# The expert's label read once per sequence on the sync engine's queue, in place of four times

## The reference

```python
x = x + L0(x)   # y = einsum('bnh,boh->bno', x, W[subject]) + b[subject]
x = x + L1(x)   # zX * second difference along features + zY * the same along tokens + zR * x * (1 - x)
x = x + L2(x)   # attention: 16 heads of 16, side input as queries, keys and values of x and one own key, then Wo
x = x + L3(x)   # experts, below
```

```python
s0 = relu(x @ swi[0]) @ swo[0]              # two shared experts, the same for every sequence
s1 = relu(x @ swi[1]) @ swo[1]
wi_sel = wi[type_label]                     # the chosen expert: one of five, its label is 0 to 2 here
wo_sel = wo[type_label]
h = relu(einsum('bsd,bdf->bsf', x, wi_sel)) # 256 x 1024
eo = einsum('bsf,bfd->bsd', h, wo_sel)      # 1024 x 256
w = softmax(relu(concat(eo[:, 0], s0[:, 0], s1[:, 0]) @ g1) @ g2)
return eo * w[0] + s0 * w[1] + s1 * w[2]
```

## Time and profile before

| | |
|---|---|
| Time, median of 3 runs | 972.61 us (971.57 to 976.15) |
| The profiled execution | 973.26 us |
| Its span in the profile | 971.4 us |
| Mean granted TensorE clock | 0.979 of full speed |
| Busy: TensorE / ScalarE / VectorE / GpSimd | 95% / 77% / 76% / 64% |
| DMA: mean rate | 154 GB/s |

### The profile page before, as it was taken

One profiled execution on the slowest core, in us unless ns is written; L12 is line 12 of the kernel. 1 busy time (PEld: TensorE's weight loads), 2 busy tenths in 40 slices (PEclk: granted clock), 3 DMA queues, 4 the chain that ended last, 5 costly groups with the idle time before them and its releaser, 6 DMA issues.

```text
span 971.4 us, 28400 instructions
## 1 busy us (share of the span) xinstructions
PE 923.5 (95%) x9138; PEld 891.7 (92%) x9138; DVE 734.1 (76%) x1518; ACT 751.3 (77%) x1682; POOL 625.1 (64%) x576
## 2 busy tenths in 40 slices
PE   8788999999999999999999999999999999999897
PEld 7688899999999999999999999999999999998897
DVE  6775777868877787887878788787878878788554
ACT  4777869688796978979697887969788796979552
POOL 4877657676675767667576766758666675866440
PEclk9999999999999999999999999999999999999999
DMA  6998867666677676667666676776767677676930
GB/s 189 199 175 189 141 174 152 157 157 132 180 154 176 138 159 160 135 173 155 179 141 157 157 140 173 149 174 152 157 157 140 173 151 176 149 157 124 148 94 11
DMA packets 361503, 149.47 MB, mean 154 GB/s; under 512 B 282340, under 2 KB 360452, under 8 KB 361476
## 3 DMA queue, kind: packets, MB, share of 16 engines
q1 hardware_dynamic: 361044, 148.74, 68.3%
q10 hardware_dynamic: 432, 0.39, 0.1%
HBM read 52.59 MB, written 4.20 MB: 58 GB/s over the span
## 4 chain that ended last, share of the span: by engine, by line
PE 62%; SPq 11%; DVE 7%; DMA 7%; ACT 6%; issue 5%; POOL 2%; ACTq 0%; DVEq 0%
PE out L760 7%; PE out L761 7%; PE out L762 7%; PE hid L760 6%; PE hid L762 6%; PE hid L761 6%; SPq L629 5%; PE front L760 4%; PE front L762 4%; PE front L761 4%; PE front L870 3%; DMA ksT<-parts_own 3%; DMA turned_own<-parts_own 3%; ACT prob_own L1131 3%; PE pv L827 2%
## 5 line engine op out<-in xcount | busy, mean ns | idle before, releaser
L1649 POOL TENSOR_TENSOR parts_own<-prob_own,parts_own 128x512 f16<-128x512 f32 x133 | 158.0, 1188 | 133.2 <-ACT parts_own L1137 133.0
L760 PE MATMUL hid<-x_hi,exp_hi 128*128 128x256 f32 x768 | 232.8, 303 | 5.5 <-DVE x_lo L1422 5.4
L1315 DVE TENSOR_REDUCE neg_max<-front 128x2 f32<-128x512 f32 x244 | 164.8, 687 | 85.3 <-PE front L870 82.8
L760 PE MATMUL out<-hid_hi,exp_hi 128*128 128x256 f32 x768 | 226.1, 294 | 2.3 <-ACT e_out L1160 2.3
L762 PE MATMUL hid<-x_hi,exp_lo 128*128 128x256 f32 x768 | 221.8, 289 | 0.0
L761 PE MATMUL hid<-x_lo,exp_hi 128*128 128x256 f32 x768 | 221.7, 289 | 0.0
L761 PE MATMUL out<-hid_lo,exp_hi 128*128 128x256 f32 x768 | 214.1, 279 | 0.0
L762 PE MATMUL out<-hid_hi,exp_lo 128*128 128x256 f32 x768 | 214.0, 279 | 0.0
L1131 ACT ACTIVATE prob_own<-front,neg_max 128x256 f32<-128x256 f32 x476 | 198.0, 482 | 13.0 <-DVE neg_max L1315 9.9
L1579 POOL TENSOR_TENSOR exp_lo<-raw,exp_hi 128x512 fp32r<-128x512 f32 x128 | 170.7, 1345 | 26.5 <-ACT exp_hi L1153 26.5
L1426 DVE SCALAR_TENSOR_TENSOR hid_lo<-hid,hid_hi 128x512 fp32r<-128x512 f32 x192 | 130.6, 686 | 48.0 <-ACT hid_hi L1175 45.8
(11 more groups left out here) (268 smaller groups left out, 2173.1 us busy)
## 6 DMA issues: line engine op xcount, KB each, us to landing
raw<-in_wi SPq DMA_DIRECT2D x64, 256.0 KB, 3.8
raw<-in_wo SPq DMA_DIRECT2D x64, 256.0 KB, 2.9
q_rows<-w_raw SPq DMA_DIRECT2D x80, 128.0 KB, 3.7
k_rows<-x_raw SPq DMA_DIRECT2D x48, 128.0 KB, 2.4
k_rows<-x1T SPq DMA_DIRECT2D x45, 128.0 KB, 2.4
x_raw<-in_x SPq DMA_DIRECT2D x16, 256.0 KB, 3.3
w_raw<-in_w SPq DMA_DIRECT2D x16, 256.0 KB, 2.7
s_raw<-in_side SPq DMA_DIRECT2D x16, 256.0 KB, 3.5
```

Of the source, the lines that this page charges most:

```text
L760: nc.tensor.matmul(acc, w_hi, a_hi, start=first, stop=False)
L1315: nc.vector.tensor_reduce(neg_max[:, :, h:h + 1], psum, AX_X, ALU.max, negate=True).then_inc(max_done, 1)
L1649: nc.gpsimd.tensor_tensor(of_head[:, 2 * S:4 * S], slot_of(prob, more_prob, i, h), of_head[:, 0:2 * S], ALU.subtract).then_inc(prob_split_ ...
```

## The change

A name `label` is added ahead of T0 in SP's list of the loop and of the closing part, and `label.15` ahead of the last sequence's wo0. It reads the label into a register and keeps it in a dictionary, under the sequence's number, or under None inside the loop. wo0 to wo3 take the register from there. wi_load goes on reading for itself, since it belongs to another sequence in the same turn.

```diff
 SP_BODY = """
-T0 T1 wo0 T2 wo1 T3 T4 T5 wo2 T6 T7 wo3 T8 T9 T10 T11 T12 T13 T14 T15 wi_load kp k3 load sum
+label T0 T1 wo0 T2 wo1 T3 T4 T5 wo2 T6 T7 wo3 T8 T9 T10 T11 T12 T13 T14 T15 wi_load kp k3 load sum
 """.split()
@@
 CLOSE_SP = list(closing("""
-T0 T1 T2 T3 T4 wo0 wo1 wo2 T5 T6 T7 T8 T9 wo3 T10 T11 T12 T13 T14 T15 wi_load wo0.15 wo1.15 sum wo2.15 wo3.15 sum.15
+label T0 T1 T2 T3 T4 wo0 wo1 wo2 T5 T6 T7 T8 T9 wo3 T10 T11 T12 T13 T14 T15 wi_load label.15 wo0.15 wo1.15 sum wo2.15 wo3.15 sum.15
 """))
@@
+            chosen = {}
+
@@
+                elif name == "label":
+                    chosen[i if isinstance(i, int) else None] = chooser(label_sb, i, wo.shape[0])
                 elif name[0:2] == "wo":
                     n = int(name[2])
-                    kind = chooser(label_sb, i, wo.shape[0])
                     wait(sp, w_split, PARTS, i, SHARED_POOL + n + 1)
-                    load_wo(kind, n)
+                    load_wo(chosen[i if isinstance(i, int) else None], n)
```

## The result

| | before | after |
|---|---|---|
| Median | 972.09 us (970.94 to 976.15, 4 runs) | 949.22 us (948.98 to 949.95, 4 runs) |
| The profiled execution, its span | 973.26, 971.4 us | 949.20, 947.3 us |
| Mean granted TensorE clock in it | 0.979 | 0.984 |

The ratio is 0.9759, 95% interval 0.973 to 0.9788: the kernel got some 23 us faster. The forecast was 958, the range 954 to 967.

The account below looks back on a forecast made before the run. TensorE, busy 95% of the span, was taken to lose time waiting for transposes behind SP's label reads. V2 12.3, P4 2.3, first loop turn 0.4 and closing turn 0.6 sum to 15.6 us off 973.26: forecast 958 us, range 954 to 967.

Parts of the forecast that it names:

- the second term: P4 on TensorE in the loop: its waits for ScalarE's e_out go, 2.3 us, between 0 and 2.3.
- the closing term: Closing turn: T5, behind wo0 to wo2, starts earlier but is held by E5; 0.6 us, between 0 and 1.5.
- the clock: TensorE's half-clock stretches: up to 1.7 us each, seven counted; two more or fewer are 3.4 us either way.
- The added read: Label read ahead of T0: hidden under SP's wait for E0, costed at 0, at worst 1.4 us.
- the first term: V2 in the loop: its wait for T2's transposed tile goes, 12.3 us, between 0 and 15.4.
- A: Rival: the DMA queue gives part back, T2's landing grows to 4.3 us; 8.9 us gained, 964.4 us; chance 0.13.
- B: Rival: V2's gain turns into later TensorE waits for ScalarE or GpSimd; 9.4 us gained, 963.9 us; chance 0.09.
- C: Rival, slower: T2's landing goes from 3.60 to 5.0 us in every loop turn; 977.6 us; chance 0.04.
- D: Rival: nothing moves, as the compiler keeps a read or something else held T2; 973 us; chance 0.06.

Follow-up runs that it names:

- e1: The kernel after, but in the loop wo1 to wo3 read the label for themselves again, so only wo0's read is gone; 953.23 us, ratio 0.9788.
- e2: The kernel after, but the loop's one read stands between T1 and wo0 instead of ahead of T0; 964.85 us, ratio 0.9907.
- e5: The kernel before with the read ahead of wo0 done twice in the loop turns; 980.41 us, ratio 1.008.
- E0: Not a run but a GpSimd step in the kernel's loop, whose end T0 waits for; no kernel e0 was run or timed.
- e3: The kernel before with all its reads, but T2 issued ahead of wo0 in the loop; 984.61 us, ratio 1.0105.
- e7: The kernel after with T2 issued ahead of wo0 in the loop; 950.92 us, ratio 0.9761.
- e6: The kernel after with T5 issued ahead of wo0 to wo2 in the closing turn; 950.15 us, ratio 0.9742.
- e4: The loop of the kernel after with the closing part of the kernel before, its reads included; 950.40 us, ratio 0.9768.

## Why the prediction came out as it did

Three steps failed, all toward too little: the second term (P4's wait), which was sized at 2.3 us and measured 4.2; the closing term, sized at 0.6 with T5 held by E5, where the reads gave 1.9; and the clock, which stood in the sum at nothing and makes 3.6 us between the two profiled executions, part of it by luck.

**Right.** The read between T1 and T2 is what V2 waited for: T2 starts 2.34 us after T1 (forecast 2.3 to 2.4), close behind E2 (0.25 us, forecast 0.17), lands in 3.7 us (forecast 3.5 to 3.8), and V1-V2 fell by 10.3 us in 13 turns and 0.65 in the first, 11.0 where the first term said 12.3. e1, e2 and e5 show it from three sides: taken away alone, put back alone, and doubled. The added read costs nothing that shows: T0 starts as close behind E0 as before. The floor of about 600 ns under such a load (the Trainium skill, "DMA: Bandwidth & Descriptors", section "Latency and other measured facts") is again not what is seen: e5's second load took 0.27 us.

**The rivals.** A, the landing that grows, came in small. In the loop T2's landing rose from 3.49 to 3.68 us where A had 4.3, and V1-V2 is 1.74 us after where e1, with a landing of 3.53, has 0.68: some 1.1 us given back. That T2 can't pass wo0 in the queue no run shows as such; they show a landing of 3.1 us ahead of wo0 (e3, e7) and 3.5 to 3.7 behind it. In the closing turn T5 behind three loads went from 4.33 to 5.74 us, and with the loads behind it (e6) to 3.1. B didn't happen: TensorE has no new wait between V2 and P5. Neither did C or D.

**Too small: the second term.** I took P4's wait as 2.3 us in 6 turns from TensorE's own view. What the change took away there was 0.32 us a turn in the mean of 13 turns, 4.2 us. The step that failed is a correction that I made for V2 (the modelled end of a matmul covers part of the wait) and left out for P4, where it covered all of it in most turns. Together the two terms make 1.11 us a turn where I had 0.88 + 0.16 = 1.04, and the turn gave 1.18: in the 13 turns 15.3 us against 13.6.

**Too small: the two turns at the ends.** The first loop turn gave 4.1 us against 1.4 (0.88 + 0.16 + 0.4), the closing turn 3.4 against 0.6, together 5.5 of the 8.5 that are missing. In the first loop turn the reads' own part was about right, 1.6 us at the V groups; 1.3 came by the clock and 1.2 at scores pairs, where kernels with the same loop differ as much. In the closing turn I had T5 held by E5 until 897.30. That was a row misread: the VectorE step at 896.62 is E7. E5 is this one, done at 892.43:

```profile
891.47 0.96 DVE L1329 TENSOR_TENSOR parts_own<-x1T,parts_own 128x512 f16<-128x512 f32 x1
```

T5 was free to take all that the reads gave, 1.9 us by e4. The other 1.5 us there are the clock fall behind V5 that went.

**The clock.** I called it a width, either way alike, at 1.7 us a fall, and counted seven falls, those that follow an x3T. There are two more between the opening and the last part: at 83.9 us in the first loop turn and behind V5 in the closing turn. Both went. What a fall costs depends on what TensorE finds behind it. One that starts at x3T puts TensorE 1.1 to 1.5 us behind the turns without one, but from 8 us after x3T on it is only 0.8 to 0.9 behind: the rest is taken back ahead of the first scores pair, where 0.78 us pass start to start in a turn without a fall and 0.12 to 0.22 in one with it. So such a fall lengthens the turn by 0.8 us (the same difference in before, after, e1, e2, e4, e6 and e7; 0.5 in e5). Falls with no such gap behind them cost 1.3 (first loop turn), 1.5 (V5) and 1.6 us (e3). In direction the clock leaned one way: the profile of after has 9 falls in all where before has 12, worth 0.8 in the 13 turns, 1.3 in the first and 1.5 in the closing one, 3.6 us of the 24.1. Which single falls went is partly luck. e2, e3 and e5 have none in the first loop turn either, and e3 and e5 none behind V5, though they keep the reads there; in the 13 turns e4, e6 and e7 have 4 and 5 with nearly the same loop as after, which has 6; and before was profiled 1.2 us above its median, so that the medians differ by 22.9 us and not 24.1. That there are fewer falls on the whole is more than luck, though single runs overlap (before has some of up to 0.987): the mean clock over all runs is 0.977 to 0.981 in the three kernels in which V2 waits (before, e2, e5) and 0.985 to 0.988 in the five in which neither V2 nor V3 does. That added waits bring falls to their own place, e3 shows. Why fewer waits at V2 leave fewer falls at x3T, half a turn away, no run shows; it stays open.

Sum of what was short: 1.7 in the 13 turns (P4 over the forecast, V2 under it), 3.6 for the three falls, 1.3 for the reads of the closing turn, 0.2 for those of the first, 1.2 at its scores pairs and 0.4 in the opening, 8.4 us; 15.6 + 8.4 = 24.0. The last 1.6 us are not shown to come from the change, nor is it shown that these very three falls went by it.

## What to carry to other kernels

A label, index or flag that a queue of DMA issues needs is to be read ahead of the first issue that somebody waits for: here, with its check, it cost 0.55 to 1.1 us each time, the engines' busy shares didn't show it, and TensorE paid it one for one where a transpose stood behind it. When a wait is sized from TensorE's rows, read the gap from start to start, or take the weight loads' view: P4's wait of 0.2 us at 446.07 doesn't appear among TensorE's at all. And price the turns at the loop's ends by themselves; two of them gave 31% of the difference here, 2.8 of their 7.5 us by clock falls that went.

## What the runs showed beside it

- A stretch of 3.4 us at half clock costs 0.8 us of a 56 us turn where a gap of TensorE follows that it can shrink, and 1.3 to 1.6 us elsewhere.
- A wait of 3.1 us at V5 was followed by such a stretch in the closing turn of before; waits of 2.0 to 2.5 us there (e3, e4, e5) were not.
- The landing of a transpose issued behind three loads of 256 KB was 5.7 us, ahead of them 3.1; in e6 the next transpose, then behind them, took 5.9.
- T2's landing differs with its neighbours in SP's list: 3.1 us ahead of wo0, 3.5 behind it with a read between T2 and wo1, 3.6 to 3.7 without that read.
